# Attention stage: the residual add of x moves to ScalarE and GpSimd, GpSimd sums two keys' products, and all engines get a new order

## The reference, cut to what matters

```
t  = 1x1 conv(group norm(x)) + pe            # one token per image and pixel, 64 channels
q2, k2, v2 = projections of layernorm(t)     # 8 heads of 8 channels
attn = softmax(q2 k2' / sqrt(8))             # 8 x 8 per pixel and head
t  = attn v2 @ wout + bout + t
tn2 = layernorm(t)
m  = (tn2 @ w1 + b1) * gelu(t @ w2 + b2) @ w3
out = 1x1 conv(m + t) + cob + x              # "+ x" is the residual that the change moves
```

## Time and profile before

| | |
|---|---|
| median of 3 executions | 1180.02 us (1178.37 to 1180.29) |
| profiled execution, its own time | 1180.53 us |
| its span, first to last instruction | 1178.7 us |
| PE busy over the span | 1077.6 us, 91% |
| DVE busy | 1066.1 us, 90% |
| ACT busy | 646.2 us, 55% |
| POOL (GpSimd) busy | 526.7 us, 45% |
| attention stage, first load to the last write of `xs` | 55.8 to 621.1 us |

### The profile page before, as it was taken

How to read it: one execution, slowest core, us unless ns; L and a number is a source line. 1 busy time by engine, 2 the same in 40 slices (tenths; PEclk the granted TensorE clock), 3 DMA queues, 4 the chain that set the end, 5 groups by cost and what they waited for, 6 DMA issues and landing times. The chain is left out here.

```text
span 1178.7 us, 20995 instructions
## 1 busy us (share of the span) xinstructions
PE 1077.6 (91%) x7238; PEld 602.5 (51%) x7238; DVE 1066.1 (90%) x1490; ACT 646.2 (55%) x1518; POOL 526.7 (45%) x416
## 2 busy tenths in 40 slices
PE   3158999999999999999978999999999999999995
PEld 2036777777777777777643333333333333333331
DVE  4719999999999999999967999999999999999995
ACT  1356888898888988888632233242233232342332
POOL 4223455554555545555314345345345444444440
PEclk9998999999999999999997999999999999999998
DMA  8001011111111111110000000110003000020003
GB/s 307 27 28 32 24 38 38 29 37 29 37 37 33 32 29 37 37 37 11 19 19 1 1 1 1 36 36 2 1 1 72 1 1 1 16 57 1 1 1 72
DMA packets 87544, 35.83 MB, mean 30 GB/s; under 512 B 70209, under 2 KB 86850, under 8 KB 86930
## 3 DMA queue, kind: packets, MB, share of 16 engines
q1 hardware_dynamic: 85634, 33.81, 10.8%
q0 software_dynamic: 768, 0.33, 0.2%
q10 hardware_dynamic: 1040, 0.35, 0.1%
HBM read 26.09 MB, written 8.39 MB: 29 GB/s over the span
## 5 line engine op out<-in xcount | busy, mean ns | idle before, releaser
L1054 PE MATMUL acc<-mixed,cwp 128*128 128x512 f32 x768 | 355.5, 608 | 4.4 <-DVE mixed L1115 2.9
L1054 PEld LDWEIGHTS acc<-mixed,cwp 128*128 128x128 f32 x768 | 140.0, 191 | 218.6 <-issue 214.9
L1072 ACT ACTIVATE y<-acc,cols 128x1024 f32<-128x1024 f32 x96 | 112.0, 1215 | 249.3 <-PE acc L1064 249.3
L1064 PE MATMUL acc<-mixed,cwp 64*64 64x512 f32 x1536 | 184.2, 600 | 11.5 <-POOL mixed L1115 11.5
L813 POOL TENSOR_TENSOR rstd<-var,half 128x8 f32<-128x8 f32 x32 | 81.8, 2556 | 221.5 <-DVE var L704 221.5
L493 DVE TENSOR_TENSOR prod<-qkv 128x1024 f32<-128x1024 f32 x128 | 155.6, 1219 | 7.3 <-POOL qkv L709 7.3
L503 DVE TENSOR_TENSOR prod<-attn,qkv 128x1024 f32<-128x1024 f32 x128 | 155.0, 1235 | 1.1
L1114 POOL TENSOR_TENSOR mixed<-xs 128x256 f32<-128x256 f32 x92 | 83.1, 903 | 156.7 <-DVE xs L1103 156.7
L1080 DVE TENSOR_TENSOR y<-y,acc 128x512 f32<-128x512 f32 x192 | 120.5, 678 | 16.3 <-ACT y L1072 16.3
L535 PE MATMUL cb<-consts,prod 128*128 128x128 f32 x1024 | 133.2, 279 | 0.0
L554 PE MATMUL cb<-consts,prod 128*128 128x128 f32 x1024 | 128.2, 273 | 2.3 <-DVE prod L503 1.6
(11 more groups left out here) (165 smaller groups left out, 1548.1 us busy)
## 6 DMA issues: line engine op xcount, KB each, us to landing
xs<-in_x SPq DMA_DIRECT2D x4, 2048.0 KB, 16.5
xa<-in_x SPq DMA_DIRECT2D x32, 256.0 KB, 2.8
xr<-in_x SPq DMA_DIRECT2D x64, 128.0 KB, 2.9
out_y<-xs SPq DMA_DIRECT2D x32, 256.0 KB, 4.6
cw<-in_L_conv_w POOLq DMA_DIRECT2D x2, 144.0 KB, 4.1
consts<-in_consts ACTq DMA_DIRECT2D x1, 192.0 KB
group<-in_consts SPq DMA_DIRECT2D x1, 64.0 KB
w1n<-in_L_conv_w ACTq DMA_DIRECT2D x1, 64.0 KB
```

The lines of the kernel that those rows point to most:

```text
L1054: pe.matmul(psum[PSUM_PAIR[v, q, j]][i][:, :, :], weights(v, i, j).rearrange("p n o -> p (n o)"), mixed[v][i][:, s0:s0 + WIDE, j, :], star ...
L1064: m = pe.matmul(psum[PSUM_PAIR[v, q, j]][i][out, :, :], edge_weights(v, i, j)[rows, :], mixed[v][i][rows, s0 + near:s0 + near + WIDE, j, : ...
L1072: act.activation(pairs(y[i][q][:, :, :]), m1, ACT.Identity, bias=cols[:, (6, 8)[v]:(7, 9)[v]]).then_inc(m1_out[i][q], 1)
```

## The change

Four things change, all in `attention_block`.

- `dve_x` goes. `act_x` on ScalarE copies the convolution's result with its bias column from PSUM to `xs`, and `pool_x` on GpSimd then adds `xr` to it in place in SBUF. TensorE's `pe_a` waits for the copies (`x_out`) in place of `x_done`; `sp_xr` waits for `x_done` as before, which GpSimd now raises.
- `pool_pair2`: for block 3 of `dve_p2` GpSimd adds the products of key 7 to those of key 6 in place (128x512), and `pe_av` makes four transposes for that block where it made eight.
- The pipeline has stages 0 to 6 where it had 0 to 4, so `run` makes 38 iterations.
- All four engines and the DMA queue have a new order within an iteration.

The helpers:

```diff
@@ -456,6 +456,9 @@
         scaled_out, scoresT_out = sem("scaled_out"), sem("scoresT_out")
         z_out, z1_out, sq2_out, cen2_out, exp_out = sem("z_out"), sem("z1_out"), sem("sq2_out"), sem("cen2_out"), sem("exp_out")
         qkv_mm, squares_out, raw_out = [[sem(f"{n}{g}") for g in range(2)] for n in ("qkv_mm", "squares_out", "raw_out")]
+        PAIRED2 = (3,)
+        paired2 = {b: sem(f"paired2_{b}") for b in PAIRED2}
+        x_out = [sem(f"x_out{d}") for d in range(2)]
         gelu_out = [sem(f"gelu_out{e}") for e in range(2)]
         var1_done, smax_done, shift_done = sem("var1_done"), sem("smax_done"), sem("shift_done")
         den_done, rden_done, biased, p1_dve = sem("den_done"), sem("rden_done"), sem("biased"), sem("p1_dve")
@@ -549,10 +552,12 @@
             if b == 0:
                 wait(pe, var2_done, t)
             wait(pe, p2_dve, DUOS * t + b + 1)
-            for j in (2 * b, 2 * b + 1):
+            if b in PAIRED2:
+                wait(pe, paired2[b], t + 1)
+            for j in (2 * b,) if b in PAIRED2 else (2 * b, 2 * b + 1):
                 for p in range(PAIRS):
                     m = pe.matmul(b4[:, TILE * p:TILE * (p + 1)], prod2[:, j, P * p:P * (p + 1)], ident,
-                                  start=(j == 0 and p == 0), stop=(j == B - 1 and p == PAIRS - 1), is_transpose=True)
+                                  start=(j == 0 and p == 0), stop=(j >= 6 and p == PAIRS - 1), is_transpose=True)
             m.then_inc(av_mm, 1)
 
         def pe_z1(pe, t):
@@ -600,8 +605,8 @@
 
         def pe_a(pe, t):
             wait(pe, tn2_done, t + 1)
-            wait(pe, x_done[0], t)
-            wait(pe, x_done[1], t)
+            wait(pe, x_out[0], t)
+            wait(pe, x_out[1], t)
             for e in range(2):
                 pe.matmul((b5, b7)[e][:, :], top["w1T"][half(e), :], tn2[half(e), :], start=True, stop=True).then_inc(a_mm, 1)
 
@@ -798,14 +803,23 @@
 
             return xr[k % 2][:, 4 * d:4 * d + 4, :]
 
-        def dve_x(dve, t, k, d):
+        def act_x(act, t, d):
+            wait(act, cow_mm, t + 1)
+            act.activation(x_view(t, d), x_psum(d), ACT.Identity, bias=cols[:, 4:5]).then_inc(x_out[d], 1)
+
+        def pool_x(pool, t, k, d):
 
             if isinstance(t, int):
-                dve.wait_ge(xr_in[k % 2], 32 * (t // 2 + 1))
+                pool.wait_ge(xr_in[k % 2], 32 * (t // 2 + 1))
             else:
-                dve.wait_ge(xr_in[k % 2], (t - k % 2) * 16 + 32)
-            wait(dve, cow_mm, t + 1)
-            dve.scalar_tensor_tensor(x_view(t, d), x_psum(d), cols[:, 4:5], xr_view(k, d), ALU.add, ALU.add).then_inc(x_done[d], 1)
+                pool.wait_ge(xr_in[k % 2], (t - k % 2) * 16 + 32)
+            wait(pool, x_out[d], t + 1)
+            pool.tensor_tensor(x_view(t, d), x_view(t, d), xr_view(k, d), ALU.add).then_inc(x_done[d], 1)
+
+        def pool_pair2(pool, t, b):
+
+            wait(pool, p2_dve, DUOS * t + b + 1)
+            pool.tensor_tensor(prod2[:, 2 * b, :], prod2[:, 2 * b, :], prod2[:, 2 * b + 1, :], ALU.add).then_inc(paired2[b], 1)
 
         def pool_rstd1(pool, t):
             wait(pool, var1_done, t + 1)
```

The orders (the lines taken out are those of the iteration functions printed above, and are left out here):

```diff
@@ -830,130 +844,130 @@
...
         def pe_iteration(pe, t, k, tiles):
+            if tiles[5]:
+                pe_g(pe, t - 5, (k - 5) % RING)
+            if tiles[1]:
+                pe_qkv(pe, t - 1, (k - 1) % RING, 0)
+            if tiles[3]:
+                pe_scores_t(pe, t - 3, 0)
+            if tiles[5]:
+                pe_var2(pe, t - 5)
+            if tiles[3]:
+                pe_scores_t(pe, t - 3, 1)
+                pe_scores_t(pe, t - 3, 2)
+                pe_scores_t(pe, t - 3, 3)
+            if tiles[6]:
+                pe_out(pe, t - 6, 0)
+                pe_out(pe, t - 6, 1)
+            if tiles[1]:
+                pe_qkv(pe, t - 1, (k - 1) % RING, 1)
+            if tiles[6]:
+                pe_cow(pe, t - 6, (k - 6) % RING)
+            if tiles[3]:
+                pe_scores(pe, t - 3)
+            if tiles[4]:
+                pe_av(pe, t - 4, 0)
+                pe_av(pe, t - 4, 1)
+                pe_av(pe, t - 4, 2)
+                pe_av(pe, t - 4, 3)
+            if tiles[5]:
+                pe_rstd2(pe, t - 5)
             if tiles[0]:
                 pe_t(pe, t, k)
+            if tiles[4]:
+                pe_z1(pe, t - 4)
+            if tiles[5]:
+                pe_a(pe, t - 5)
+            if tiles[4]:
+                pe_center(pe, t - 4, (k - 4) % RING)
+
+        def act_iteration(act, t, k, tiles):
+            if tiles[1]:
+                act_t(act, t - 1, (k - 1) % RING)
+            if tiles[5]:
+                act_square2(act, t - 5)
+                act_centered(act, t - 5)
             if tiles[2]:
+                act_scale(act, t - 2, (k - 2) % RING)
             if tiles[1]:
                 act_squares(act, t - 1, 0)
                 act_raw(act, t - 1, (k - 1) % RING, 0)
+            if tiles[5]:
+                act_gelu(act, t - 5, 1)
+                act_rrep(act, t - 5)
+            if tiles[3]:
+                act_scores_t(act, t - 3)
+            if tiles[1]:
+                act_squares(act, t - 1, 1)
+                act_raw(act, t - 1, (k - 1) % RING, 1)
+            if tiles[5]:
+                act_gelu(act, t - 5, 0)
+            if tiles[6]:
+                act_x(act, t - 6, 1)
+                act_x(act, t - 6, 0)
+            if tiles[4]:
+                act_z(act, t - 4)
             if tiles[3]:
                 act_exp(act, t - 3)
+
+        def dve_iteration(dve, t, k, tiles):
+            if tiles[5]:
+                dve_p2(dve, t - 5, (k - 5) % RING, 2)
+                dve_p2(dve, t - 5, (k - 5) % RING, 3)
             if tiles[4]:
+                dve_max(dve, t - 4)
+                dve_shift(dve, t - 4)
+            if tiles[2]:
+                dve_var1(dve, t - 2)
+            if tiles[3]:
+                dve_p1(dve, t - 3, (k - 3) % RING, 0)
+                dve_p1(dve, t - 3, (k - 3) % RING, 1)
+            if tiles[6]:
+                dve_tn2(dve, t - 6)
+            if tiles[5]:
+                dve_z1(dve, t - 5, (k - 5) % RING)
+            if tiles[6]:
+                dve_gated(dve, t - 6, 0)
             if tiles[4]:
+                dve_sum(dve, t - 4)
+                dve_reciprocal(dve, t - 4)
+                dve_attn(dve, t - 4)
+            if tiles[6]:
+                dve_gated(dve, t - 6, 1)
+            if tiles[3]:
+                dve_p1(dve, t - 3, (k - 3) % RING, 2)
+            if tiles[5]:
+                dve_var2(dve, t - 5)
+            if tiles[3]:
+                dve_p1(dve, t - 3, (k - 3) % RING, 3)
             if tiles[4]:
+                dve_p2(dve, t - 4, (k - 4) % RING, 0)
+                dve_p2(dve, t - 4, (k - 4) % RING, 1)
         def pool_iteration(pool, t, k, tiles):
+            if tiles[6]:
+                pool_x(pool, t - 6, (k - 6) % RING, 0)
             if tiles[0]:
                 pool_rstd1(pool, t)
+            if tiles[5]:
+                pool_x(pool, t - 5, (k - 5) % RING, 1)
+            if tiles[3]:
+                pool_rstd2(pool, t - 3)
+            if tiles[0]:
+                pool_bias(pool, t, k)
+            if tiles[2]:
+                pool_pair2(pool, t - 2, 3)
         def sp_iteration(sp, t, k, tiles):
             if 0 <= t - -1 < TILES:
                 sp_xa(sp, t + 1, k + 1)
+            if tiles[6]:
+                sp_xr(sp, t - 6, k - 6)
         def run(eng, iteration):
+            for t in range(TILES + 7 - 1):
+                iteration(eng, t, t % RING, [0 <= t - s < TILES for s in range(7)])
         block = ctx.enter_context(nc.Block())
```

More of the change, by code:

```diff
@@ L833, in pe_iteration @@
+            if tiles[1]:
[11 more added lines that the diff above has]
+                pe_rstd2(pe, t - 5)
             if tiles[0]:
                 pe_t(pe, t, k)
-            if tiles[2]:
-                pe_scores_t(pe, t - 2, 3)
@@ L837, in pe_iteration @@
[L837 to L869, removed]
@@ L870, in pe_iteration @@
-            if tiles[4]:
-                pe_cow(pe, t - 4, (k - 4) % RING)
-        def act_iteration(act, t, k, tiles):
+            if tiles[4]:
[10 more added lines that the diff above has]
+                act_centered(act, t - 5)
+            if tiles[2]:
+                act_scale(act, t - 2, (k - 2) % RING)
@@ L877, in act_iteration @@
+            if tiles[4]:
+                act_z(act, t - 4)
             if tiles[3]:
                 act_exp(act, t - 3)
+        def dve_iteration(dve, t, k, tiles):
+            if tiles[5]:
+                dve_p2(dve, t - 5, (k - 5) % RING, 2)
+                dve_p2(dve, t - 5, (k - 5) % RING, 3)
             if tiles[4]:
[L880 to L883, removed]
-            if tiles[4]:
-                act_gelu(act, t - 4, 1)
@@ L939, in pool_iteration @@
+            if tiles[6]:
[6 more added lines that the diff above has]
+                dve_p1(dve, t - 3, (k - 3) % RING, 3)
```

(19 more changed lines are left out.)

## The result

The changed kernel takes 1245.2 us at the median of 4 runs (1244.31 to 1246.89); beside it the kernel before took 1180.15 (4 runs). The ratio is 1.0555 [1.0537, 1.0573]: 5.6% slower. The profiled execution took 1246.9 us, with a span of 1245.0. In the changed kernel's lines L496 is p1, L506 p2, L714 the bias add, L822 the pair add, L817 the residual adds of x, L808 ACT's copies, L611 `pe_a`, L559 the attention transposes, L595 the sums for var2.

A forecast was written before the change was run, and what follows sets the result against it. PE set the 16.28 us period, DVE right behind. DVE's new period 15.13 + 2.15 + 0.42 + 0.6 = 18.3; 28 x (18.3 - 16.28) = 56.6, plus 4, on 1180.0 gives 1240.6, said as 1240, range 1206 to 1257.

The forecast's parts named there:

- The bias add, 2.15 a period: POOL's bias add lands among DVE's p2 products and p2(2) stands for 2.15 us per period, bounds 0 and 2.34.
- The single example of the earlier trace: One p2 during pipeline fill took 3.37 us against a 1.22 median beside a bias add; source of the 2.15 price.
- Rival 1: POOL's adds don't block DVE's products and PE goes on setting the pace: 1170 us, chance 0.10.
- x(0) on p1(0), 0.42: POOL's x(0) add, behind the pair add, stalls DVE's p1(0) by 0.42 us per period, bounds 0 and 0.61.
- Rival 2: Only the bias add costs; x(0)'s stall and the var2 wait vanish: 1212 us, up to 1229 with one left; chance 0.22.
- The pair add, 1.19: POOL's 128x512 pair add takes 1.19 us, bounds 0.61 and 2.34, and just fits beside DVE's max and shift.
- Rival 3: The pair add takes 1.75 us, outlasts max and shift and stalls further DVE instructions: 1265 us, chance 0.10.
- The wait of 0.6: DVE waits 0.6 us per period at var2 for PE, whose way from tn2 is longer; bounds 0 and 0.9.
- the sign that I named for it: DVE idle some 0.6 us ahead of var2, waiting for PE L590.
- DVE's own 15.13 and PE's 0.45: DVE's own work falls to 15.13 us per period without its x instructions; PE gains 0.45 from four fewer transposes.
- ACT's copies, 0.33 each: ACT's two 128x256 copies out of PSUM take 0.33 us each, bounds 0 and 0.60, and cost nothing.
- Fill and drain, 4 in all: Filling and draining the attention pipeline add 2 us each, bounds for both together -5 and +8.

The follow-up runs named there:

- e1: Changed kernel with GpSimd's bias add cut to the first two columns of each image's q (128x16 in place of 128x1024); 1181.9 us, 1.001.
- e4: Changed kernel with the bias added to q alone, half the columns (128x512); 1210.4 us, 1.0257.
- b6: Kernel before with one more GpSimd add of 128x512 on a scratch buffer behind the bias add, nothing waiting for it; 1198.6 us, 1.0163.
- e3: Changed kernel with GpSimd's x(0) moved behind rstd1; 1230.6 us, 1.0426.
- e5: Changed kernel without the pair add (eight transposes again) and with x(0) behind rstd1; 1233.1 us, 1.0445.
- e6: Changed kernel with x(0) behind rstd1 and the bias added to q alone; 1197.0 us, 1.0147.
- e2: Changed kernel without the pair add, PE back to eight transposes in block 3; 1257.0 us, 1.0651.
- b5: Kernel before in its old order with x(1) and the pair add moved behind p2(3), full bias add on q and k behind the pair; 1199.0 us, 1.0159.

## Why the prediction was right, step by step

**The bias add, 2.15 a period: right**, in place (p2(2), rstd2 of 2.56 ahead of it) and size (3.37 less 1.22). The single example of the earlier trace rows was enough. e1 takes the stall away and 63 us with it, e4 halves it, b6 makes another one out of an add that nobody needs. Rival 1 falls with these. That POOL goes ahead of DVE's next product is seen at 320.00, where the waiting add goes and p2(2), issued at 319.92, stands.

**x(0) on p1(0), 0.42: right**, measured at 0.45 on the two p1 and at 0.52 a period by e3. Rival 2 was the changed kernel with one or both of the small stalls gone; e3 is that kernel without x(0)'s and gives 1230.6, where the rival said up to 1229. The prediction calls two SBUF inputs of the DVE instruction the condition; e1's var1, with one, stands too.

**The pair add, 1.19: 0.07 to 0.08 too small.** It takes 1.26 and 1.27. It ran from 324.51 to 325.77, shift ended at 325.81, and x(0) behind it fell onto p1(0) as forecast. Rival 3, in which it would take 1.75, has nothing for it.

**The wait of 0.6: right in size, at another instruction.** It stands at gated(0), 0.56 us for PE's `pe_a` (23 times, 12.8 us, between 130 and 560), and not at var2, where DVE never waits in that stretch; the sign that I named for it didn't come. I added up two ways from tn2 to var2, 6.2 for PE and 5.6 for DVE, and took the difference at their end. Both lengths are right: tn2 starts at 328.53, and PE's L595 ends 6.19 later; DVE starts var2 6.27 later, of which 0.56 is the wait and 5.71 the rest. But `pe_a` can't start before tn2 ends, and in the new order DVE has only z1 to do before gated(0) needs it; before, two p1 products lay there as well. Had DVE not waited there, it would have come to var2 at 334.24 at the latest, and PE's L595 ends at 334.72: the same time would have gone at var2, less 0.1 at most. But 0.56 is `pe_a` against z1, and not the difference that I had worked out; that the two are so nearly alike is luck. The same 0.56 stands in e1, e3, e4, e5 and e6.

**DVE's own 15.13 and PE's 0.45: right.** 15.13 + 2.15 + 0.45 + 0.56 = 18.29, against 18.37 measured. The missing 0.08 is the overlap of neighbours that an idle wait takes away: I took it out for the old wait at z1 and left it out for the new one. PE's 28 transposes take 3.22 in e1 and the 32 of e5 3.66, so four are worth 0.44. PE waits 2.25 us a period, so they buy nothing. e1 shows what the change would be worth without the large stall: 1182, with periods of 16.28 and 16.37 in turn. None of DVE's 0.79 or PE's 0.45 is left, since x(0), there on var1, and the wait at gated(0) take them.

**ACT's copies, 0.33 each: too small, at no cost.** The two take 0.88 together (L808), and ACT is busy for 80%.

**Fill and drain, 4 in all: 3 too small**, the one term that was mis-sized enough to see. p1(0) of tile 3 starts at 124.20, 3.55 later than before; one more stretched p2 than before, from 118.33, is 2.15 of it, as forecast. Tile 31's starts at 638.68, and the attention stage's last instruction ends 48.0 us later, at 686.7; before it was 44.5 (621.1 less 576.6). That is 3.5 for the drain. The last x adds wait there for ACT's copies, and the granted clock over those 48.0 us is 0.86, where it was 0.92 over the 44.5; one `pe_a` there takes 2.08 in place of 1.13. How the 3.5 divides between the longer chain and the clock no run separates.

```profile
685.50 1.23 POOL L817 TENSOR_TENSOR xs<-xs,xr 128x256 f32<-128x256 f32 x2 [5.43 <-ACT xs L808]
```

28 periods of 2.09 more are 58.5 (forecast 56.6), and with 7.1 it is 65.6 of the 66.3 by which the span grew. The rest of the kernel behind the attention stage is 0.7 longer: it carried over, as assumed.

## What to carry to other kernels

In this kernel an add on GpSimd was free only where the vector engine ran instructions that take an input from PSUM; a product with both inputs in SBUF, and in e1 even a tiny instruction on one SBUF tensor, stood for nearly the add's length. Before moving an add, write down what the vector engine does from its issue to its end, and move it into a stretch that is free or leave it. In these traces such a stall shows as a longer vector instruction and never as a wait, so compare the least and the longest of each line. Look for one stretched instruction in the fill or the drain, where the order differs from the steady state: it prices the collision before anything is built. And when an instruction is taken off a queue, ask what was held back behind it (e2), and when another is added ahead of a late one, what data is waited for behind it (b5).

## What was not expected of the hardware

- A memset of 128x1024 on POOL beside a 128x1024 product with two SBUF inputs stretches neither: 0.95 and 1.21 us.
- The stall is the add's own time less about 0.2: 2.15 for an add of 2.34, 1.03 for 1.27 (b6), 0.45 for 0.63 (the shortest x add). The product's end comes 1.08 after the add's end in all three cases of a 128x1024 product looked at.
- An add of only 128x16 takes 0.21 us on POOL in the first two tiles and 0.87 when it is issued beside the p2 products, which it doesn't stretch (e1). The 128x8 rstd is alike: 1.64 alone, 2.55 beside products, and no product is longer for it.
- A DVE instruction with a single SBUF input, var1 of 128x8, goes from 0.16 to 0.63 us beside a POOL add (e1).
- After idle stretches of 1.77 us the clock granted to PE fell to its lower level in some periods and not in others (e2: 20.0 and 18.4 us); with 1.56 us it stayed at 1.00 from 130 to 600 us (e5).
